# Four chained attention layers on one core: pieces of work moved between slots, and three tiles of one sum given to PE

## The chip, the cores and the metric

One core of a Trainium2 chip runs one program on 8 images. The metric is the device time of the execution in microseconds (us); lower is better. Before the change three runs took 3123.68, 3125.5 and 3131.82 us.

## The reference, cut to what matters

Each image (256 channels, 32x32 = 1024 positions) passes through four layers, numbered 0 to 3.

```python
# layer 0: group norm (32 groups), q, k, v; per head a 32x32 attention over channels
attn = softmax(einsum('bhcn,bhdn->bhcd', q, k) * 32 ** -0.5); x = x + proj(attn @ v)
# layer 1: one head, 32 channels of q and k, 128 of v, 1024x1024 attention over positions
o = einsum('oi,bihw->bohw', Wo, softmax(q^T k) applied to v) * gamma + x
# layers 2 and 3: group norm (8 groups), 8 heads of 32 channels, 1024x1024 attention per head
attn = softmax(q^T k * 32 ** -0.5); out = proj(attn @ v) + bias
# layer 2 adds its input, layer 3 adds its normalised input
```

All is float32. The softmax's maximum over each row is computed, split into two bfloat16 halves and subtracted inside the score product.

## The kernel before, in words

**Data.** The images go through one after the other. `xa` holds the image in layers 0 to 2, `scratch` in HBM is its copy between layers 1 and 2 (`save`, L640; `reload`, L643), `xb` the one that becomes layer 3's input. `Q` and `K` hold per head three stacked parts of 32 rows (high, high, low; and high, low, high), so that one fp32r product of 96 rows gives the float32 score, and 8 more rows of `Q` for the maxima.

**Groups.** Layers 2 and 3 have 4 groups each per image: 4 heads times one half (512) of the queries; layer 1 has 2. `LAST3` (4) is layer 3 of the last image. A group has 8 steps (one tile of 128 keys each) of 4 heads, that is 32 slots. In a slot PE makes one score tile of 128x512 (L1244) in one of two PSUM banks, ACT turns it into `prob` with exp (L874); after four slots PE multiplies the step's four tiles by v into the values bank (L1269), one step behind the scores. The softmax's sums: POOL adds the step's tiles into `acc` (L770), PE multiplies `acc` by ones (L1289) in `finish`. Tiles from `pooled(layer, g)` on are not added by POOL: `finish` multiplies them by ones itself (L1285), all of them before it waits for `acc`. `invert` (DVE) and `scale` (POOL, L748) follow.

**Maxima.** Ahead of a group's scores its row maxima are needed: 32 more score products (L1213; `max`) into three PSUM banks, each reduced by DVE (L997), then `split` on DVE (L1003 to L1011) and `maxrow`: a product on PE (L1220), a copy on ACT (L848) and a DMA that puts the rows into `Q` (L686). The first score of the group waits for it (L1236). They are laid beside the slots of the group before.

**Pieces.** Everything else is a piece: `side` products with a side bank of PSUM each (two banks in turn), `stats`, `norm`, `power`, `apply` of the group norms, `stack`, `save`, `load`, `store`. A q or k piece is `("side", layer, "qk", m, i)`: four PE products in two halves (`begin` and `side`, L1157), ACT's `hi` (L822), DVE's `lo` (L964), then `stack` on SP: three DMAs of 256 KB from `hi` and `lo` into `Q` or `K` (L674), four stacks for two heads groups' q and k. ACT's `hi` waits until the last stack of the same half i has landed (L815), the first maxima of a group with new stacks wait for all of them (L1204). m = 0, 1 are the early pieces, m = 2, 3 the late ones. `side(layer, "mean")` (L1064) is the product that spreads the moments over the group norm's groups: DVE's `stats` and `norm`, then ACT's moments (L836) in `norm`, then this product, then three DVE operations (L937), POOL's `power` (L727), ACT's `apply` (L794).

**Order.** `group_sequence` writes the order by hand. An entry is (layer, g, pieces with their slot, maxima). Maxima (layer, g, start, stop, low, high) are spread over slots low to high, `rows(layer, g, slot)` is a maxrow. `spread(first, last, pieces)` deals cut pieces evenly over slots; `at` gives slots one by one; `gap` is a stretch without scores. `plans` unrolls this into one list per turn, and every engine runs its own part of this list in its order, with semaphores between them. Turns: image 0 up to layer 1 and layer 2's first maxima (`first`), image 0's layer 2 with image 1's layers 0 and 1 between (`second`), `third` (one group), six times `steady`, `last`.

Of the kernel before, what the change touches and what calls it, by code (L numbers as in the profile page):

```python
# [16 lines left out]
T = C // P  # L17
# [4 lines left out]
NQ = N // QW  # L22
KC = N // P
# [12 lines left out]
LAST3 = 4  # L36
# [33 lines left out]
def normalise(layer):  # L70
    return ([("stats", layer, t, i) for t in range(T) for i in range(NQ)]
            + [("norm", layer), ("side", layer, "mean"), ("power", layer)]
            + [("apply", layer, t, i) for t in range(T) for i in range(NQ)])
# [7 lines left out]
def side(layer, what, n):  # L81
    return [("side", layer, what, i) for i in range(n)]
# [14 lines left out]
def after_layer1(rest=True):  # L97
    more = split_operand(2, 0) + split_operand(2, 1) + side(2, "v", KC // 2)
    return side(1, "out", T * NQ) + [("save",)] + normalise(2) + (more if rest else [])


def chunks(piece):

    if piece[0] != "side":
        return 1
    return {"qk": T, "v": T, "v0": 2, "v1": 2, "out": 1 if piece[1] == 1 else T, "gram": KC, "keys": T, "mix": T}.get(piece[2], 1)


def beside(pieces, others):

    return [x for i, piece in enumerate(pieces)
            for x in [piece] + others[i * len(others) // len(pieces):(i + 1) * len(others) // len(pieces)]]


def cut(pieces):

    return [x for piece in pieces for x in [("begin", c) + piece[1:] for c in range(chunks(piece) - 1)] + [piece]]


def spread(first, last, pieces):  # L120

    pieces = cut(pieces)
    return [(first + (last - first) * (2 * i + 1) // (2 * len(pieces)), x) for i, x in enumerate(pieces)]


def group_sequence():
    end = LAST_PIECE
    out2, out3 = side(2, "out", T * NQ), side(3, "out", T * NQ) + [("store", 3)]
    out1 = after_layer1(False)
    early2, late2 = (split_operand(2, m) + split_operand(2, m + 1) for m in (0, 2))  # L130
# [4 lines left out]
    def at(slots, pieces):  # L135
        return [*zip(slots, pieces)]

    def gap(pieces):
        return (None, None, pieces, [])

    def rows(layer, g, slot):
        return (layer, g, None, None, slot, slot)
# [21 lines left out]
    def layer2_begins(pieces):  # L164
# [3 lines left out]
    early_halves, late_halves = (side(2, f"v{half}", KC // HPT) for half in range(T))  # L168
    maxima2 = [("max", 2, 0, a) for a in range(MAXIMA[2])]
    first = [gap([("load",)] + channel_attention(True) + rest0 + split_operand(1, 0) + side(1, "v", 2))] + layer1 \  # L170
        + [gap(cut(out1 + early2) + beside(cut(side(2, "v", KC // 2)), maxima2) + [("split", 2, 0), ("maxrow", 2, 0)])]
    chain0 = channel_attention(True)[len(normalise(0)):] + rest0 + split_operand(1, 0) + side(1, "v", 2)
    second = [(2, 0, [(0, ("load",))] + spread(0, 14, late2)
               + at((9, 10, 11, 12, 13, 15, 16, 18, 19, 20, 21), normalise(0)) + spread(22, 32, chain0[:6]),
               [(2, 1, 0, 32, 0, 23), rows(2, 1, 27), (2, 2, 0, 8, 24, 31)]),
              (2, 1, spread(0, 26, chain0[6:]),
               [(2, 2, 8, 32, 0, 17), rows(2, 2, 19), (1, 0, 0, 8, 24, 27), rows(1, 0, 31), (1, 1, 0, 8, 28, 31)]),
              (1, 0, [], [rows(1, 1, 3), (2, 3, 0, 8, 0, 7)]),
              (1, 1, [], [(2, 3, 8, 16, 0, 7)]),
              (2, 2, at((12, 13, 14, 15, 16), out1[:T * NQ + 1])  # L180
               + at((17, 17, 18, 18, 19, 21, 24, 28, 29, 30, 31), out1[T * NQ + 1:]),
               [(2, 3, 16, 32, 0, 15), rows(2, 3, 19)]),
              (2, 3, spread(0, 14, early2) + spread(14, end, early_halves),
               [(2, 0, 0, 32, 14, 29), rows(2, 0, 31)])]
    third = [(2, 0, [(0, ("reload",))] + spread(0, 14, late2) + spread(14, 18, late_halves) + spread(18, end, out2),
              [(2, 1, 0, 32, 0, 23), rows(2, 1, 27), (2, 2, 0, 8, 24, 31)])]
    steady = (layer2(True, True)
# [2 lines left out]
                   (3, 1, 16, 24, 24, 31)]),  # L190
                 (1, 0, [], [(3, 1, 24, 32, 0, 7)]),
                 (1, 1, [], [rows(3, 1, 3), (3, 2, 0, 8, 0, 7)]),
                 (3, 1, at((12, 13, 14, 15, 16), out1[:T * NQ + 1])
                  + at((17, 17, 18, 18, 19, 21, 24, 28, 29, 30, 31), out1[T * NQ + 1:]),
                  [(3, 2, 8, 32, 0, 23), rows(3, 2, 27), (3, 3, 0, 8, 24, 31)]),
                 (3, 2, spread(0, 20, early2), [(3, 3, 8, 32, 0, 23), rows(3, 3, 27), (2, 0, 0, 8, 24, 31)]),
                 (3, 3, spread(0, end, side(2, "v", KC // 2)),
                  [(2, 0, 8, 32, 0, 23), rows(2, 0, 27), (2, 1, 0, 8, 24, 31)]),
                 (2, 0, spread(0, 14, late2) + spread(SCALED, end, out3),
# [2 lines left out]
            for x in (("side", LAST3, "out", ot * NQ + i), ("store", LAST3, ot * NQ + i))]  # L202
    half_out4 = len(out4) // NQ
    early4, late4 = (split_operand(LAST3, m) + split_operand(LAST3, m + 1) for m in (0, 2))
# [2 lines left out]
                [(3, 1, 8, 32, 0, 23), rows(3, 1, 27), (3, 2, 0, 8, 24, 31)]),  # L207
               (3, 1, at((1, 2, 3, 4, 5, 8, 11, 15, 16, 17, 18), normalise(LAST3)),
                [(3, 2, 8, 32, 0, 23), rows(3, 2, 27), (3, 3, 0, 8, 24, 31)]),
               (3, 2, spread(0, 20, early4), [(3, 3, 8, 32, 0, 23), rows(3, 3, 27), (LAST3, 0, 0, 8, 24, 31)]),  # L210
               (3, 3, spread(0, end, side(LAST3, "v", KC // 2)),
                [(LAST3, 0, 8, 32, 0, 23), rows(LAST3, 0, 27), (LAST3, 1, 0, 8, 24, 31)]),
               (LAST3, 0, spread(0, 14, late4) + spread(SCALED, end, out3),
# [85 lines left out]

def pooled(layer, g):  # L300

    return KC - 1 if layer != 2 and g > 0 or layer == LAST3 or (layer, g) == (2, 1) else KC


# [1036 lines left out]
```

## Time and profile before

| | |
|---|---|
| median of three runs | 3125.5 us |
| the profiled execution, and its span | 3135.67 us, 3133.9 us |
| busy: PE, POOL, DVE, ACT | 2853.4, 2187.9, 1857.8, 1553.1 us |
| PE, costliest lines (busy) | L1244 scores 1085.1, L1213 maxima 834.3, L1269 values 577.8 us |
| POOL, L770 sums | 1721.4 and 312.6 us |
| DVE, L997 maxima | 1411.3 us |
| DMA queue | 148.56 MB, 31.2% of 16 engines |

Times are from the start of the span. A slot's time is taken from the start of its score on PE. The profile's list of waits has for every engine and line what ended its idle time, the total, the number of times and the longest. The clock is TensorE's granted clock: 1.00 is 2.4 GHz, 0.50 is 1.2 GHz.

### The profile page before, as it was taken

The page shows a single profiled execution, that of the slowest core. Times are in us where ns is not written, and L with a number is a line of the kernel's source. Part 1 is how long each engine was busy: PE and PEld are TensorE (multiplying, and loading weights), DVE is VectorE, ACT ScalarE, POOL GpSimd, SP SyncE. Part 2 cuts the span into 40 slices and gives each one's busy share as a digit, 9 for nine tenths or more (in the row PEclk, how much of TensorE's full clock was granted, in tenths as well). Part 3 has the DMA queues.
Part 4 walks back from the last instruction along what each step waited for, and adds up shares of the span by engine and source line. Part 5 has one row for each costly group of instructions (what it writes and reads, how often), then busy time and mean ns, then how long its engine had stood idle before and what let it go on. Part 6 is the DMA issues. An engine that isn't in the chain of part 4 may idle for free.

```text
span 3133.9 us, 36186 instructions
## 1 busy us (share of the span) xinstructions
PE 2853.4 (91%) x13136; PEld 1415.3 (45%) x13136; DVE 1857.8 (59%) x3293; ACT 1553.1 (50%) x2794; POOL 2187.9 (70%) x748
## 2 busy tenths in 40 slices
PE   6668979999999989999999999999899998999997
PEld 4235434554445444454445544454344544444442
DVE  1254547566674666656675666756666566767672
ACT  1224445455564455544554545545556445555554
POOL 3215657677785777768776777867777586798877
PEclk8779889999999999999999999999999999999999
DMA  2160044333340334321343323413334123333330
GB/s 69 28 83 12 16 61 69 39 49 51 46 84 13 42 56 69 56 42 25 43 83 43 52 35 47 89 23 43 56 42 83 26 42 42 56 56 43 42 57 15
DMA packets 74388, 150.87 MB, mean 48 GB/s; under 512 B 9121, under 2 KB 10657, under 8 KB 74210
## 3 DMA queue, kind: packets, MB, share of 16 engines
q1 hardware_dynamic: 74210, 148.56, 31.2%
q8 instruction: 104, 1.70, 0.3%
q14 instruction: 74, 0.61, 0.1%
HBM read 20.46 MB, written 16.78 MB: 12 GB/s over the span
## 4 chain that ended last, share of the span: by engine, by line
PE 64%; DMA 9%; ACT 8%; DVE 7%; POOL 6%; issue 3%; SPq 2%; ACTq 0%; POOLq 0%; DVEq 0%
PE psum L1244 14%; PE psum L1269 11%; PE psum L1213 10%; POOL acc L770 6%; PE psum L1188 5%; PE psum L1157 5%; DMA Q<-lo 5%; PE psum L1165 4%; ACT prob L874 4%; PE psum L1265 3%; DVE maxpart L997 3%; DMA K<-hi 2%; PE psum L1090 2%; PE psum L1289 2%; DMA Q<-max_rows 2%
## 5 line engine op out<-in xcount | busy, mean ns | idle before, releaser
L997 DVE TENSOR_REDUCE maxpart<-psum 128x1 f32<-128x512 f32 x2176 | 1411.3, 684 | 857.3 <-PE psum L1213 835.0
L770 POOL TENSOR_TENSOR acc<-acc,prob 128x2048 f32<-128x2048 f32 (+1 forms) x447 | 1721.4, 3851 | 233.5 <-ACT prob L874 194.2
L874 ACT ACTIVATE prob<-psum 128x512 f32<-128x512 f32 x2176 | 1225.1, 596 | 1012.2 <-PE psum L1244 971.8
L1244 PE MATMUL psum<-Q,K 104*128 104x512 f32 x2048 | 1085.1, 532 | 77.8 <-ACT prob L874 55.2
L1213 PE MATMUL psum<-K,Q 96*128 96x512 f32 x2048 | 834.3, 411 | 72.4 <-DMA K<-hi 60.0
L1244 PEld LDWEIGHTS psum<-Q,K 104*128 104x128 f32 x2048 | 393.7, 193 | 780.6 <-ACT prob L874 447.6
L770 POOL TENSOR_TENSOR acc<-prob 128x2048 f32<-128x2048 f32 (+1 forms) x80 | 312.6, 3907 | 586.6 <-PE psum L1289 457.8
L1269 PE MATMUL psum<-prob,vT 128*32 128x512 f32 x4096 | 577.8, 624 | 0.0
L1213 PEld LDWEIGHTS psum<-K,Q 96*128 96x128 f32 x2048 | 401.3, 196 | 208.3 <-issue 132.4
L1269 PEld LDWEIGHTS psum<-prob,vT 128*32 128x32 f32 x4096 | 100.6, 110 | 205.6 <-ACT prob L874 122.9
L1157 PE MATMUL psum<-ha,wqkv_sb 128*128 128x512 f32 x288 | 152.0, 619 | 9.9 <-ACT ha L794 9.9
L1188 PE MATMUL psum<-att,wp_sb 128*128 128x512 f32 x256 | 131.1, 600 | 3.4 <-POOL att L748 3.4
L748 POOL TENSOR_TENSOR att<-att,turned_sums 128x512 f32<-128x512 f32 x80 | 102.1, 1276 | 28.9 <-DVE turned_sums L1025 28.9
L1157 PE MATMUL psum<-hb,wqkv_sb 128*128 128x512 f32 x224 | 120.0, 623 | 0.0
L964 DVE SCALAR_TENSOR_TENSOR lo<-psum,cols_sb,hi 128x512 fp32r<-128x512 f32 x64 | 48.1, 751 | 121.3 <-ACT hi L822 121.3
L1265 PE MATMUL psum<-prob,products 128*128 128x512 f32 x256 | 118.8, 608 | 0.0
L1289 PE MATMUL psum<-acc,ones 128*32 128x512 f32 x640 | 86.1, 610 | 15.3 <-POOL acc L770 15.3
L853 ACT COPY att<-psum 128x512 f32<-128x512 f32 x80 | 47.0, 587 | 88.3 <-PE psum L1265 52.8
L1021 DVE STREAM_TRANSPOSE turned_sums<-psum 128x512 f32<-128x512 f32 x80 | 56.5, 707 | 53.0 <-PE psum L1289 52.8
L822 ACT ACTIVATE hi<-psum,cols_sb 128x512 fp32r<-128x512 f32 x64 | 44.0, 688 | 80.3 <-DMA Q<-lo 50.4
L964 DVE SCALAR_TENSOR_TENSOR lo<-psum,hi 128x512 fp32r<-128x512 f32 x64 | 44.2, 690 | 66.5 <-ACT hi L822 66.1
L1265 PEld LDWEIGHTS psum<-prob,products 128*128 128x128 f32 x256 | 47.5, 192 | 61.7 <-issue 59.9
(117 smaller groups left out, 1970.7 us busy)
## 6 DMA issues: line engine op xcount, KB each, us to landing
Q<-hi SPq DMA_DIRECT2D x128, 256.0 KB
K<-hi SPq DMA_DIRECT2D x128, 256.0 KB
Q<-lo SPq DMA_DIRECT2D x64, 256.0 KB
K<-lo SPq DMA_DIRECT2D x64, 256.0 KB
xa<-in_x SPq DMA_DIRECT2D x8, 1024.0 KB, 8.4
scratch<-xa SPq DMA_DIRECT2D x8, 1024.0 KB, 4.0
xb<-scratch SPq DMA_DIRECT2D x8, 1024.0 KB, 4.9
out<-hb SPq DMA_DIRECT2D x7, 1024.0 KB, 5.7
```

Source lines behind the costliest of these rows:

```text
L748: pool.tensor_tensor(dst, dst, turned_sums[:, :, :].rearrange("p a c -> p (a c)"), ALU.mult).then_inc(group_done, 1)
L770: pool.tensor_tensor(total, first if a == 1 else total, this, ALU.add).then_inc(added, 1)
L874: act.activation(prob[STEP_STARTS.slot(b, start)][:, j, :], score_bank[(SCORES.rank[b.n][e] - 1) % SCORE_BANKS], ACT.Exp, scale=1.0 if lay ...
L997: dve.tensor_reduce(maxpart[layer][:, a // NQ, a % NQ:a % NQ + 1], bank, AX_X, ALU.max).then_inc(max_free, 1)
L1157: ins = pe.matmul(side_bank, wqkv_sb[layer][:, t, o:o + P], normed[layer][:, t, part], start=(t == 0), stop=(t == T - 1))
L1165: ins = pe.matmul(side_bank[:, a * width:(a + 1) * width], src[:, t, kt * P:(kt + 1) * P], w[:, t, o:o + width], start=(t == 0), stop=(t = ...
L1188: ins = pe.matmul(side_bank, w[:, t, ot * P:(ot + 1) * P], src[:, t, part], start=(t == 0), stop=(t == T - 1))
L1213: pe.matmul(max_bank[(r - 1) % MAX_BANKS], left, right, start=True, stop=True).then_inc(max_full, 1)
L1244: pe.matmul(score_bank[(r - 1) % SCORE_BANKS], left, right, start=True, stop=True).then_inc(score_full, 1)
L1265: ins = pe.matmul(values_bank, vT1[:, kt, :], slot[:, j, :], start=(kt == 0), stop=(kt == KC - 1))
L1269: ins = pe.matmul(values_bank[head_rows(j), :], vT[layer][:, s, head * DH:(head + 1) * DH], slot[:, j, :], start=(s == 0), stop=(s == KC - 1),
L1289: ins = pe.matmul(side_bank[head_rows(j), :], ones[:, :], acc[:, 0 if layer == 1 else j, :], start=(not own), stop=True, tile_position=(0, ...
```

## The change

Four things are moved in the hand-written order, and one function is changed.

- **Turn `first`**: ahead of the first maxima now stand all of layer 2's v pieces and the first late q piece with its stack; between the maxima three more stand (of m = 2 and 3) instead of v, and the last one (m = 3, i = 1) between `split` and `maxrow`, its stack behind it.
- **Turn `second`**: group (2,0) has no late pieces any more, and the normalisation of image 1 begins at slot 6 instead of 9. In (2,1) layer 0's chain and layer 1's pieces end at slot 23 instead of 26, the first maxima of layer 1 stand at slots 27 to 30 instead of 24 to 27, those of (1,1) move into (1,0). The maxima of (2,3) move one group later (8 in (1,1), 24 in (2,2)). In (2,3) early pieces and v halves end at slot 18, the maxima stand at 17 to 30 instead of 14 to 29.
- **`steady`**: in (3,1) layer 1's four output pieces and `save` stand one slot later, the means' product at slot 23 instead of 21, `power` at 25 instead of 24; in (3,2) the early pieces are dealt over slots 1 to 15 instead of 0 to 20. In the last image's (3,2) over 0 to 14.
- **`pooled`**: 5 instead of 7 for the last group of all, so that `finish` sums its tiles 5, 6 and 7 on PE.

```diff
     first = [gap([("load",)] + channel_attention(True) + rest0 + split_operand(1, 0) + side(1, "v", 2))] + layer1 \
-        + [gap(cut(out1 + early2) + beside(cut(side(2, "v", KC // 2)), maxima2) + [("split", 2, 0), ("maxrow", 2, 0)])]
+        + [gap(cut(out1 + early2 + side(2, "v", KC // 2) + late2[:2]) + beside(cut(late2[2:6]), maxima2)
+               + [("split", 2, 0)] + cut(late2[6:7]) + [("maxrow", 2, 0), late2[7]])]
     chain0 = channel_attention(True)[len(normalise(0)):] + rest0 + split_operand(1, 0) + side(1, "v", 2)
-    second = [(2, 0, [(0, ("load",))] + spread(0, 14, late2)
-               + at((9, 10, 11, 12, 13, 15, 16, 18, 19, 20, 21), normalise(0)) + spread(22, 32, chain0[:6]),
+    second = [(2, 0, [(0, ("load",))]
+               + at((6, 7, 8, 9, 10, 12, 14, 17, 18, 19, 20), normalise(0)) + spread(22, 32, chain0[:6]),
                [(2, 1, 0, 32, 0, 23), rows(2, 1, 27), (2, 2, 0, 8, 24, 31)]),
-              (2, 1, spread(0, 26, chain0[6:]),
-               [(2, 2, 8, 32, 0, 17), rows(2, 2, 19), (1, 0, 0, 8, 24, 27), rows(1, 0, 31), (1, 1, 0, 8, 28, 31)]),
-              (1, 0, [], [rows(1, 1, 3), (2, 3, 0, 8, 0, 7)]),
-              (1, 1, [], [(2, 3, 8, 16, 0, 7)]),
+              (2, 1, spread(0, 23, chain0[6:]),
+               [(2, 2, 8, 32, 0, 17), rows(2, 2, 19), (1, 0, 0, 8, 27, 30), rows(1, 0, 31)]),
+              (1, 0, [], [(1, 1, 0, 8, 0, 3), rows(1, 1, 7)]),
+              (1, 1, [], [(2, 3, 0, 8, 0, 7)]),
               (2, 2, at((12, 13, 14, 15, 16), out1[:T * NQ + 1])
                + at((17, 17, 18, 18, 19, 21, 24, 28, 29, 30, 31), out1[T * NQ + 1:]),
-               [(2, 3, 16, 32, 0, 15), rows(2, 3, 19)]),
-              (2, 3, spread(0, 14, early2) + spread(14, end, early_halves),
-               [(2, 0, 0, 32, 14, 29), rows(2, 0, 31)])]
+               [(2, 3, 8, 32, 0, 23), rows(2, 3, 27)]),
+              (2, 3, spread(0, 10, early2) + spread(10, 18, early_halves),
+               [(2, 0, 0, 32, 17, 30), rows(2, 0, 31)])]
...
-                 (3, 1, at((12, 13, 14, 15, 16), out1[:T * NQ + 1])
-                  + at((17, 17, 18, 18, 19, 21, 24, 28, 29, 30, 31), out1[T * NQ + 1:]),
+                 (3, 1, at((13, 14, 15, 16, 17), out1[:T * NQ + 1])
+                  + at((17, 17, 18, 18, 19, 23, 25, 28, 29, 30, 31), out1[T * NQ + 1:]),
...
-                 (3, 2, spread(0, 20, early2), [(3, 3, 8, 32, 0, 23), rows(3, 3, 27), (2, 0, 0, 8, 24, 31)]),
+                 (3, 2, spread(1, 15, early2), [(3, 3, 8, 32, 0, 23), rows(3, 3, 27), (2, 0, 0, 8, 24, 31)]),
...
-               (3, 2, spread(0, 20, early4), [(3, 3, 8, 32, 0, 23), rows(3, 3, 27), (LAST3, 0, 0, 8, 24, 31)]),
+               (3, 2, spread(0, 14, early4), [(3, 3, 8, 32, 0, 23), rows(3, 3, 27), (LAST3, 0, 0, 8, 24, 31)]),
...
 def pooled(layer, g):
 
+    if (layer, g) == (LAST3, T * NQ - 1):
+        return KC - 3
     return KC - 1 if layer != 2 and g > 0 or layer == LAST3 or (layer, g) == (2, 1) else KC
```

`out1` is layer 1's four output pieces, `save` and layer 2's normalisation (4 stats, norm, mean, power, 4 applies).

## Rows read from the trace of the kernel before

**Rows 1.** The page, part 1: busy us, share of the span, instructions.
```profile
PE 2853.4 (91%) x13136; PEld 1415.3 (45%) x13136; DVE 1857.8 (59%) x3293; ACT 1553.1 (50%) x2794; POOL 2187.9 (70%) x748
```
**Rows 2.** Waits of PE, whole span: total us, times, longest us.
```profile
PE psum L1213 <- DMA K<-hi: 60.0, 10, 15.1
PE psum L1244 <- ACT prob L874: 58.4, 120, 3.0
PE psum L1064 <- ACT mv L836: 29.8, 10, 12.0
```
**Rows 3.** Timeline of PE, turn 3: start us, us, work [idle before <-releaser].
```profile
741.92 0.36 PE L1064 MATMUL psum<-mv,const_sb 128*128 128x4 f32 x2 [2.12 <-ACT mv L836]
...
788.13 0.77 PE L1213 MATMUL psum<-K,Q 96*128 96x512 f32 x1 [4.68 <-DMA K<-hi]
```
**Rows 4.** Timeline of PE, images 0 and 1.
```profile
176.17 2.35 PE L1213 MATMUL psum<-K,Q 96*128 96x512 f32 x4 [15.08 <-DMA K<-hi]
...
314.54 1.19 PE L1213 MATMUL psum<-qk 96*128 96x512 f32 x2 [5.77 <-DMA qk<-K]
...
428.88 1.19 PE L1213 MATMUL psum<-K,Q 96*128 96x512 f32 x2 [11.32 <-DMA K<-hi]
```
**Rows 5.** Timelines of POOL and PE at the end of the span.
```profile
3096.40 23.30 POOL L770 TENSOR_TENSOR acc<-acc,prob 128x2048 f32<-128x2048 f32 x5
...
3119.75 1.93 PE L1289 MATMUL psum<-acc,ones 128*32 128x512 f32 x8 [5.87 <-POOL acc L770]
```
**Rows 6.** Timeline of PE, finish of (3,1) in turn 3.
```profile
763.19 1.07 PE L1285 MATMUL psum<-prob,ones 128*32 128x512 f32 x8
764.07 1.04 PE L1289 MATMUL psum<-acc,ones 128*32 128x512 f32 x8
```
**Rows 7.** Windows: length, then busy us (instructions) of each engine, clock, DMA share, GB/s.
```profile
759.66:788.13 28.47, 23.27 (x110) 10.41 (x109) 17.76 (x31) 13.88 (x25) 22.41 (x6) 0.99 0.86 112
836.67:863.90 27.23, 26.43 (x114) 12.27 (x110) 18.87 (x30) 13.52 (x25) 18.18 (x5) 1.00 0.95 116
2905.77:2935.08 29.31, 23.52 (x110) 10.34 (x109) 17.58 (x31) 14.02 (x25) 27.44 (x8) 0.99 0.84 108
...
787.41:794.23 6.82, 6.10 (x21) 3.21 (x22) 2.77 (x4) 2.37 (x4) 4.75 (x2) 0.50 0.02 2
```
**Rows 8.** Timeline of ACT, (2,0) of turn 3.
```profile
845.28 0.69 ACT L822 ACTIVATE hi<-psum,cols_sb 128x512 fp32r<-128x512 f32 x1 [3.71 <-DMA Q<-lo]
```
**Rows 9.** Windows of whole groups; the engines are PE, PEld, DVE, ACT, POOL.
```profile
832.13:874.90 42.77, 41.30 (x182) 19.12 (x181) 28.65 (x47) 21.30 (x38) 32.10 (x9) 1.00 0.67 89
3021.79:3051.13 29.34, 28.85 (x149) 12.28 (x149) 22.49 (x39) 18.45 (x34) 21.01 (x6) 1.00 0.06 18
...
713.44:753.62 40.18, 35.89 (x152) 15.67 (x150) 29.94 (x55) 20.66 (x38) 37.05 (x17) 0.96 0.08 28
```
**Rows 10.** Timeline of ACT around the moments, (3,1) of turn 3.
```profile
741.11 0.67 ACT L836 ACTIVATE mv<-mv 128x1 f32<-128x1 f32 x2 [3.03 <-DVE mv L913]
741.68 2.35 ACT L874 ACTIVATE prob<-psum 128x512 f32<-128x512 f32 x4
```
**Rows 11.** Timeline of POOL, behind power.
```profile
744.57 9.26 POOL L770 TENSOR_TENSOR acc<-acc,prob 128x2048 f32<-128x2048 f32 x2
```
**Rows 12.** Windows of images 0 and 1: the gap's wait, (2,0), (2,2), behind (2,3)'s gate.
```profile
159.00:176.17 17.17, 2.08 (x5) 1.21 (x5) 0.75 (x1) 0.69 (x1) 0.00 (x0) 0.50 0.95 112
...
202.85:251.86 49.01, 43.26 (x176) 21.91 (x176) 32.05 (x57) 26.78 (x49) 29.01 (x13) 0.89 0.58 81
...
356.36:396.44 40.08, 35.76 (x136) 13.81 (x134) 19.90 (x39) 21.60 (x40) 36.97 (x17) 0.85 0.08 28
...
428.88:459.34 30.46, 25.15 (x125) 13.81 (x126) 20.79 (x36) 11.50 (x20) 22.75 (x5) 0.89 0.05 14
```
**Rows 13.** Timeline of DVE, the gap's maxima.
```profile
180.36 16.83 DVE L997 TENSOR_REDUCE maxpart<-psum 128x1 f32<-128x512 f32 x28 [0.91 <-PE psum L1213]
```
**Rows 14.** Timeline of SP, first issues of layer 1's stacks behind a maxrow.
```profile
304.52 1.22 SPq L666 DMA_DIRECT2D qk<-hi  x2
```

## The prediction

> **What bounds the kernel now.** TensorE is busy 91% of the span [rows 1]. A share says nothing about single stages, so I read next for whom PE waited: 60.0 us in 10 waits for K's last stacked piece, 58.4 us in 120 for softmax tiles, 29.8 us in 10 for the moments ahead of the means' product [rows 2]. PE's own timeline places them. The six middle images repeat one pattern: a wait of 2.12 us ahead of the means' product and one of 4.6 to 4.7 us ahead of the first maxima of the next layer's group 0, (3,2) slot 24; the last image has the second of the two as well [rows 3, 7]. Images 0 and 1 hold the long ones, 15.08, 5.77 and 11.32 us [rows 4]. At the end PE waits 5.87 us for POOL's sums [rows 5]. PE is the bound between the waits, so the sum is made wait by wait. The windows below are cut at a group's first score.
>
> **The tail.** POOL's five last additions take 23.30 us from 3096.40, 4.66 each, and PE's last acc products start behind them at 3119.75 [rows 5]. Two additions go: POOL ends at 3110.4. PE's last values end near 3112.8, and it now sums three tiles instead of one, 0.88 us each (763.19 to 764.07 [rows 6]): 2.6 us. The acc products start at 3115.5 without a wait and run at 0.88 instead of 1.93: everything behind them is 5.1 us earlier, and a little of the low clock that stretched the last output products may go too. **-5.5 us** (-3 to -7).
>
> **Early q and k pieces, (3,2) of the middle images.** The 4.68 us are a wait for data. Four stacks of 768 KB lie between the first issue at 759.66 and the first maximum at 788.13: 28.47 us at 112 GB/s, DMA share 0.86. The late pieces of (2,0), spread over 14 slots as the early ones will be, run at 116 GB/s and 0.95 [rows 7]. The transfer can't be shortened, only its gap closed: 3.15 MB at 116 GB/s are 27.1 us, 1.3 less. The first issue moves little, since the first piece's second half stays in slot 2; the 0.76 us for which its first half waited at slot 0 is spent on slot 1's score instead. I give 0.8 for this and 0.4 for what comes earlier upstream (next paragraph): **-2.5 us** an image.
> What of the 4.68 us stays, changes place: ACT's hi of the fourth piece waits for the second stack's landing and stands in ACT's queue ahead of exponentials. In (2,0) ACT was held 3.71 us that way at 845.28 [rows 8], and PE lost little (41.30 busy of 42.77 [rows 9]), because finish and a forced piece kept it busy. In (3,2) PE has less to do there; I expect it held some 2.8 us at slots 15 to 16 and again 3 at the maxima (an estimate, on which the sum does not rest). The end is set by the stream. Bounds: 0, if the gap in the stream stays, and -7.7: the 4.68 us, and half of the 6.1 us that it runs at 1.2 GHz behind them (788.13 to 794.23 [rows 7]). Near the first, for the stream's rows say so. Six images: **-15**.
> In the last image the second half moves to slot 1, 0.9 us earlier, and its stretch, 29.31 us at 108 GB/s [rows 7], has 2.1 to close: **-3**.
>
> **The means' product, two slots later.** The diff moves PE's instruction, but ACT's moments (norm) keep slot 19. They run at 741.11 and only behind them the exponential at 741.68 [rows 10]. A score needs the exponential two before it, so PE, freed of the product, stops a score later until 742.3, when it took up its scores before too. The wait changes its name, from the moments to the tiles of prob. The output pieces a slot later save 0.6 of 1.18 us (POOL's scaled att comes when it came), the fourth passes behind a values step: 0.4 net, counted above. Cost: DVE now takes the product behind the last maximum and the four operations of the split, so POOL's power, queued ahead of the two additions of 4.63 us that ended at 753.83 [rows 11], holds these about 2.3 us. PE needs them at 764.07 [rows 6], 8 us behind that: hidden. Without this cover, 2.3 us an image.
>
> **Image 0, the gap.** In the 17.17 us ahead of the maxima PE does 2.08 us of work, at 1.2 GHz [rows 12]. All v products and a qk piece go there, some 10 to 12 us: hidden if they end by 176.2. Among the maxima (28 in 16.83 us [rows 13]) stand two lo operations in place of v, and a third piece ahead of the maxrow product: +1.8 and +0.9, less 1.5 because the first maxima no longer start at half speed. **+1.2** (-1 to +4).
> **(2,0) behind it**, 49.01 us, loses the late pieces. A half piece costs 0.76 us: (2,0) at 832.13 takes 42.77 us, with 16 halves more than the last image's (LAST3,1), 29.34, and 1.2 of idle [rows 9]. Eight are 6.1 us. With them go ACT's and DVE's waits for stacks, of the 5.75 us in which PE was not busy [rows 12] say 3.1, and 1.3 of half speed (mean clock 0.89). **-10.5**; -5 if x's load, now behind a stack, and the normalisation three slots earlier give new waits, -13 if all idle goes.
> **(2,1)**: the last stack of layer 1 has seven slots instead of two ahead of its maxima, and 14 issues of 0.6 us, the first at 304.52, set its landing [rows 14]. Of 5.77 us about 2.2 stay: -3.5. Eight maxima of 0.24 us leave for (1,0): -1.9; the split then ends just ahead of maxrow: +1. **-4.5** (-1 to -8).
> **(2,2)** takes eight maxima more, but runs at a mean clock of 0.85 now; the like group at 713.44, with all 32, takes 40.18 us at 0.96 against its 40.08 [rows 9, 12]. Less eight of 0.24, plus some clock: **-1** (-3 to +2).
> **(2,3)**: its stream has no gap to close, so its gate stays at 428.88; but three slots, a values step and three v halves (2 + 2.3 us) pass ahead of it instead of behind, where 30.46 us lay [rows 12]. DVE's floor there, 32 maxima of 0.60 [rows 13], is 19.2, and the split and row DMA behind it stay. **-4.5** (-1 to -7).
>
> **Sum**: -5.5 - 15 - 3 + 1.2 - 10.5 - 4.5 - 1 - 4.5 = -42.8 us. The profiled execution took 3135.7 us (its span 3133.9), 10 above the median of 3125.5; so 3092.9 in its terms, and 3083 for the median.
>
> **Where the clock speaks against it.** After the 4.68 us wait PE runs 6.8 us at 1.2 GHz [rows 7]. Cut in two, the wait may give two such stretches. The Trainium skill (TensorE: Matmul & The Clock Gate, HAM oscillation) says that work in bursts between DMA waits is throttled anew at each burst, to half speed. The trace agrees in direction. By that rule the split wait brings rival (a) below.
>
> **Rivals.** (a) Slower: the middle images then have three stops (the score behind the moments, slot 16, the maxima). If each draws 6.8 us at half speed, 20.5 us against 10.2 now, half of it lost, that is 5.1 more in 7 images, 36 us, with the gate unmoved; the rest keeps -24.8: +11, 3137. It decides from 3.6 us an image. For it: the 6.8 us stretch. Against: half speed ahead of a gate that DMA sets costs nothing. 4%. (b) The stream doesn't close up, as ACT's order holds the third and fourth pieces: middle and last images give 0, 3101. The rows of (2,0) speak against it. 17%. (c) Images 0 and 1 find new waits (x behind the stack, split ahead of maxrow): gap +3, (2,0) -6, (2,1) -2, (2,3) -2, that is 12.3 less: 3095. 17%. (d) Better: the stop at the gate gets too short for a low clock, 3 us in 7 images: 3062. 14%. (e) The moved pieces only rename waits everywhere and the tail alone pays: 3120, 4%. The forecast itself 44%.
> The range takes in (b), (c), (d) and the units' bounds: 3061 to 3108. Under 0.3% (9.4 us) is what this kernel's measurement can't tell from nothing. Faster by more, all but (a) and (e): 0.92; same 0.04; slower 0.04.
>
> **What would show it.** Right: K's wait in PE's list falls from 60 to 25 to 35 us and ACT's for Q's stacks grows by some 2 us an image; the moments' wait falls under 18 us while that for tiles of prob grows by about as much; from first issue to first maximum in (3,2) it is 27 us; image 0's (2,0) takes 38 us; the 5.9 us wait for acc is gone. Wrong: that stretch still 28.5 us; two low clocks in (3,2); the gap's first maxima past 178; acc late for the group after the norm.

## The result and the profile after

The changed kernel takes 3090.4 us (median of six runs, 3085.0 to 3097.0) against 3125.0 of the kernel before beside it: ratio 0.9882, 95% interval 0.9863 to 0.9900. A second series on another occasion gave 3086.0 against 3128.5, ratio 0.9864 (0.9847 to 0.9882). The forecast was 3083 with the range 3061 to 3108.

The first profiled execution of the changed kernel has a span of 3095.3 us, 38.6 less than before; that of the second series 3085.1, 48.8 less. The profiled execution before was 10 us longer than its series' median, the first one after 7 us, so the medians tell the gain (35 and 43 us) and the profiles where it lies. To read them by stage I cut both timelines of PE at the first score of each group, as in the prediction. Durations in us:

| stage | forecast | before | after | second profile |
|---|---|---|---|---|
| up to the first score, same instructions | 0 | 89.8 | 87.1 | 84.9 |
| (1,1) with the gap | +1.2 | 100.4 | 105.6 | 105.0 |
| (2,0) | -10.5 | 49.0 | 39.9 | 39.9 |
| (2,1), (1,0), (1,1) | -4.5 | 104.5 | 98.7 | 98.7 |
| (2,2) | -1 | 40.1 | 40.6 | 40.7 |
| (2,3) | -4.5 | 62.9 | 62.3 | 61.7 |
| (3,1), six middle images | 0 | 240.3 | 239.2 | 243.3 |
| (3,2), six middle images | -15 | 259.0 | 239.9 | 236.0 |
| (3,2), last image | -3 | 43.5 | 41.5 | 40.4 |
| from the last group's first score | -5.5 | 52.4 | 48.3 | 45.2 |
| sum of those that the forecast moves, against before | -42.8 | | -35.0 | -44.3 |

The two profiles of one kernel differ by up to 4.1 us in one row. In (3,1) that is TensorE's clock alone: PE is idle 24.2 us in both, and runs 20 us at 1.2 GHz in the first and 34 in the second. In (3,2) it is PE's idle time, 18.4 and 14.1 us. Single groups differ less between executions, but enough to matter for a small row: with the same instructions the old (2,3) took 62.9 to 64.4 us in four profiles (before, experiments one, two and four), the new one 60.7 to 62.3 in five (the two of the changed kernel, three, six and seven). So the sum says more than its parts.

PE's busy time hardly moves; what goes is its waiting. The page's first part of the changed kernel, to be held against [rows 1]:

```profile
PE 2858.6 (92%) x13152; PEld 1411.0 (46%) x13152; DVE 1857.5 (60%) x3293; ACT 1552.5 (50%) x2794; POOL 2178.9 (70%) x746
```

Its list of PE's waits (total us, times, longest), to be held against [rows 2], and under it that of ACT, both over the whole span:

```profile
PE psum L1247 <- ACT prob L877: 75.7, 125, 2.7
PE psum L1216 <- DMA K<-hi: 18.5, 10, 3.7
PE psum L1067 <- ACT mv L839: 18.4, 3, 11.7
PE psum L1247 <- DMA Q<-max_rows: 13.9, 16, 5.2
```
```profile
ACT hi L825 <- DMA Q<-lo: 108.8, 45, 6.9
```

The wait for K's last piece falls from 60.0 to 18.5 us (11.8 in the second profile), that for the moments from 29.8 to 18.4, and that for tiles of prob grows by 17.3. ACT waited 85.1 us for Q's stacks before.

### The profile page after: what moved, and what is told of

It reads as the page before. It is cut to its first block, busy times and chain, and to the rows that moved or that the text cites. A ratio compares the mean times of both kernels' runs of the same rounds, so it can differ in the third digit from the quotient of the medians.

```text
span 3095.3 us, 36215 instructions
## 1 busy us (share of the span) xinstructions
PE 2858.6 (92%) x13152; PEld 1411.0 (46%) x13152; DVE 1857.5 (60%) x3293; ACT 1552.5 (50%) x2794; POOL 2178.9 (70%) x746
## 4 chain that ended last, share of the span: by engine, by line
PE 64%; DMA 12%; ACT 8%; DVE 7%; POOL 3%; issue 3%; SPq 2%; ACTq 0%; POOLq 0%; DVEq 0%
PE psum L1247 15%; PE psum L1272 11%; PE psum L1216 10%; DMA Q<-lo 7%; PE psum L1191 6%; PE psum L1160 5%; ACT prob L877 4%; PE psum L1168 4%; PE psum L1268 4%; DVE maxpart L1000 3%; POOL acc L773 3%; DMA K<-hi 3%; PE psum L1093 2%; DMA Q<-max_rows 2%; DVE stats L909 2%
## 5 line engine op out<-in xcount | busy, mean ns | idle before, releaser
L1216 PE MATMUL psum<-K,Q 96*128 96x512 f32 x2048 | 838.5, 413 | 35.4 <-DMA K<-hi 18.5
L1292 PE MATMUL psum<-acc,ones 128*32 128x512 f32 x640 | 87.3, 617 | 12.7 <-POOL acc L773 8.6
L730 POOL TENSOR_TENSOR rstd<-gvar,half_power 128x2 f32<-128x2 f32 x24 | 16.8, 699 | 93.8 <-DVE gvar L942 93.8
```

The costliest lines, as they stand in the source:

```text
L1216: pe.matmul(max_bank[(r - 1) % MAX_BANKS], left, right, start=True, stop=True).then_inc(max_full, 1)
```

## Experiments

Each gives its edit, then what was on record, then what came. In each the kernel before ran on the same chip, 3126.0 us in the first four, 3128.5 in the next four, 3129.0 in the last three.

**One: early pieces alone**, in the kernel before.

```diff
-  (3, 2, spread(0, 20, early2), [(3, 3, 8, 32, 0, 23), rows(3, 3, 27), (2, 0, 0, 8, 24, 31)]),
+  (3, 2, spread(1, 15, early2), [(3, 3, 8, 32, 0, 23), rows(3, 3, 27), (2, 0, 0, 8, 24, 31)]),
...
-  (3, 2, spread(0, 20, early4), [(3, 3, 8, 32, 0, 23), rows(3, 3, 27), (LAST3, 0, 0, 8, 24, 31)]),
+  (3, 2, spread(0, 14, early4), [(3, 3, 8, 32, 0, 23), rows(3, 3, 27), (LAST3, 0, 0, 8, 24, 31)]),
```


> The kernel before with only the early q and k pieces dealt over slots 1 to 15 (steady) and 0 to 14 (last image). My theory (the end is set by the data stream of four stacks, whose gap closes, and a shorter wait leaves less time at 1.2 GHz): first issue to first maximum in (3,2) falls from 28.5 to 27.3 us, the group takes 3 us less in each of the 7 images, the total falls by 18 to 24 us, ACT's hi is held about 2.5 us for the fourth piece. Rival (half of it comes from the output pieces and the means' product that stand one and two slots later): the group gains under 1.5 us an image, the total under 11 us. Rival (the clock eats it): two low clocks in (3,2) and the total within 5 us of before.

Measured: 3111.3 us, ratio 0.9948 (0.9931 to 0.9966), 16 us. The six groups (3,2) took 234.7 us, 24.3 less, the last 3.4 less; PE's wait for K was 36.3 us. So the early pieces are the largest part, and with 27.7 us by stage larger than the forecast's 18. The total is less than the 18 to 24 us expected of this run: its profiled execution is 5 us shorter than its median and the one before 10 us longer than its own, so the stages say more than the medians bear out. The rival that gave half of the gain to the output pieces is out: they are not moved here.

**Two: the means' product alone**, in the kernel before.

```diff
-  (3, 1, at((12, 13, 14, 15, 16), out1[:T * NQ + 1])
-   + at((17, 17, 18, 18, 19, 21, 24, 28, 29, 30, 31), out1[T * NQ + 1:]),
+  (3, 1, at((13, 14, 15, 16, 17), out1[:T * NQ + 1])
+   + at((17, 17, 18, 18, 19, 23, 25, 28, 29, 30, 31), out1[T * NQ + 1:]),
```


> The kernel before with only the six (3,1) groups changed: output pieces and save one slot later, means' product at slot 23, power at 25. My theory (PE's stop is ACT's norm in front of the exponentials, so the wait is only renamed): waits for the moments fall by about 12 us and waits of L1244 for prob grow by as much; (3,1) takes 0.2 to 0.5 us less an image at the same clock, the total falls by 0 to 3 us, not measurable. Rival (the product's wait is really removed): 2.1 us an image, the total falls by 12 us or more.

Measured: 3126.0 us, ratio 0.9997 (0.9986 to 1.0008): nothing. PE's waits in it, over the whole span:

```profile
PE psum L1244 <- ACT prob L874: 75.8, 129, 2.9
PE psum L1213 <- DMA K<-hi: 58.8, 10, 15.1
PE psum L1064 <- ACT mv L836: 17.1, 4, 11.7
```

Against [rows 2] the moments' wait loses 12.7 us and that for prob gains 17.4: a change of name, as expected.

**Three: images 0 and 1 alone.** The edit is the change's first hunk whole, from `first` to the end of `second`; in its kernel the pairs of lines are these and those of `second`:

```diff
-        + [gap(cut(out1 + early2) + beside(cut(side(2, "v", KC // 2)), maxima2) + [("split", 2, 0), ("maxrow", 2, 0)])]
+        + [gap(cut(out1 + early2 + side(2, "v", KC // 2) + late2[:2]) + beside(cut(late2[2:6]), maxima2)
+               + [("split", 2, 0)] + cut(late2[6:7]) + [("maxrow", 2, 0), late2[7]])]
...
```

> The kernel before with only the turns first and second changed (images 0 and 1). My theory, from the trace of after: gap +5, (2,0) -9, (2,1) and (1,0) together -6, (2,2) and (2,3) within 1 each; 10 us less in all up to the end of (2,3), and 10 +- 4 in the total. Rival (my forecast of 19 us was right and after's execution met a low clock by chance there): 16 us or more.

Measured: 3120.5 us, ratio 0.9980 (0.9969 to 0.9991), 6 us. By stage: gap with (1,1) 105.8, (2,0) 37.7, (2,1) 74.7, (2,3) 60.7 us, in sum with (1,0), (1,1) and (2,2) 10.7 less. Of the 19.3 us forecast there about half comes, as was expected of this run after the first profile; its rival, a low clock by chance, is out.

**Four: the tail alone.**

```diff
+    if (layer, g) == (LAST3, T * NQ - 1):
+        return KC - 3
```

> The kernel before with only the last group's tiles 5 and 6 moved from POOL to PE. My theory: POOL's last additions end 9.3 us earlier, PE's acc products start behind its own 2.6 us without a wait for POOL, the last group takes 4 to 5 us less, and the total falls by about 5 us, at the edge of what can be measured. Rival (the end is set by ACT's values copy and the output stores): under 2 us.

Measured: 3121.2 us, ratio 0.9983 (0.9971 to 0.9994), 5 us. PE's timeline at its end (start, us, work, idle before):

```profile
3106.14 2.76 PE L1287 MATMUL psum<-prob,ones 128*32 128x512 f32 x24
3108.72 1.04 PE L1291 MATMUL psum<-acc,ones 128*32 128x512 f32 x8
```

The acc products follow without a wait. The four parts give 16 + 1 + 6 + 5 = 28 us by their ratios, the whole 37 and 43 by its two: no sign that the parts take anything from each other. Whether they help each other stays open; each interval is 3 to 6 us to either side.

**Five: the changed kernel once more**, for the comparisons below.

> The changed kernel itself, beside its variants on one chip, so that their differences are read against it. Both theories: about 3090 us, ratio to the kernel before 0.986 to 0.990, with the stages of its first profile: steady (3,2) near 240 us for the six, (3,1) near 239, the gap with (1,1) near 105, (2,3) near 62, tail near 48.

Measured: 3086.0 us, its stages as in the table's last column; there (3,1) is 4 us above the 239 expected, (3,2) 4 below 240 and the tail 3 below 48.

**Six: the moments two slots later as well**, in the changed kernel.

```diff
-  + at((17, 17, 18, 18, 19, 23, 25, 28, 29, 30, 31), out1[T * NQ + 1:]),
+  + at((17, 17, 18, 18, 21, 23, 25, 28, 29, 30, 31), out1[T * NQ + 1:]),
```


> The changed kernel with the steady means' normalisation called two score slots later (21 instead of 19), so that ACT's moments of the mean stand behind two more exponentials. Theory 1 (the stop of 2 to 2.7 us at score slot 22 of every steady (3,1) group is ACT held in order by the mean's moments, which wait for PE's transposed sums, with exponentials queued behind them): that stop goes, the six (3,1) groups take about 227 instead of 239 us, the waits for ACT's probabilities fall by about 12 us, total about 3078. Theory 2 (the stop is only one of several equal ones, and PE is then held by the mean's own product at slot 23 or by a later exponential): (3,1) stays within 4 us of 239, the wait for ACT's mv is over 25 us, total 3087 to 3093.

Measured: 3092.3 us (3087.3 to 3093.3), ratio 0.9885 (0.9869 to 0.9901), against 0.9864 for the changed kernel beside it: no gain, and if anything 6 us more, with intervals that overlap. That is the second theory's total; its (3,1) within 4 us of 239 and its wait for the moments of over 25 us were missed narrowly (233.9 and 24.8). Its waits of PE:

```profile
PE psum L1247 <- ACT prob L877: 60.4, 121, 2.2
PE psum L1067 <- ACT mv L839: 24.8, 9, 11.6
PE psum L1216 <- DVE maxpart L1000: 18.6, 34, 1.5
```

The tiles' wait falls by 16.3 us against the 76.7 of the same kernel without the edit, and 6.4 come back at the moments, 4.9 at the maxima that stand behind DVE's part of the norm. PE is idle 0.8 us less in each (3,1), 4.6 in six. In its profile the six took 233.9 us against 243.3, but most of that is the clock: by the groups' mean clocks 10 us of the six ran at 1.2 GHz against 34. The runs' times show no gain.

**Seven: one late piece back behind the row maxima's product**, in the changed kernel's gap.

```diff
-  + [("split", 2, 0)] + cut(late2[6:7]) + [("maxrow", 2, 0), late2[7]])]
+  + [("split", 2, 0), ("maxrow", 2, 0)] + cut(late2[6:]))]
```


> The changed kernel with only this moved back: in the gap before image 0 the second of the two late q/k pieces that the change put between the first maxima stands behind the transposition of the row maxima. Theory 1 (each piece between the maxima holds DVE for 1.5 to 2 us, and its stack's DMAs stand in front of the row maxima's DMA, for whose landing PE waits 5.2 us): the gap with (1,1) is 1.5 to 3 us shorter than 105, and (2,0) loses less than 1 of it, total about 3088. Theory 2 (the gap is set by the landing of the first K stacks, and the piece only moves the waiting): gap and (2,0) together within 0.5 us.

Measured: 3098.9 us (3096.3 to 3100.8), ratio 0.9908 (0.9892 to 0.9924): 13 us slower than the changed kernel beside it. The gap with (1,1) is 3.0 us shorter, as the first theory said, and (2,0) 3.6 longer, which it did not. PE's and DVE's timelines in its (2,0):

```profile
211.19 0.80 PE L1216 MATMUL psum<-K,Q 96*128 96x512 f32 x1 [4.65 <-DVE maxpart L1000]
```
```profile
209.85 0.69 DVE L909 BATCH_NORM_STATS2 stats<-xa 128x6 f32<-128x512 f32 x1 [4.81 <-DMA xa<-in_x]
```

PE waits for a PSUM bank of the maxima, DVE's reductions stand behind the next image's statistics, and those wait for x, whose transfer was issued at 200.85 behind the moved piece's stack. What the gap gains, the next image's load takes back. Gap and (2,0) together take 145.5 us, as in the changed kernel's two profiles (145.5 and 144.8): the second theory's number, but not its mechanism, for the gap did get shorter and the wait is for x, not for the first K stacks. Nearly all of the 12 us by which this profile is longer than the changed kernel's second lies behind, in instructions that were not moved: (2,1) and (1,0) 5.2 us and the end 3.1, with 14 and 7 us more at 1.2 GHz; the groups from `third` on 5.6, where PE is idle 7.6 us longer and runs 7 us less at 1.2 GHz; (2,2) is 2.4 shorter. Why is open, so this run does not show what the piece's place is worth to the total.

**Eight: K's pieces ahead of Q's**, in the changed kernel.

```diff
-    early2, late2 = (split_operand(2, m) + split_operand(2, m + 1) for m in (0, 2))
+    early2, late2 = (split_operand(2, m + 1) + split_operand(2, m) for m in (0, 2))
-    early3, late3 = (split_operand(3, m) + split_operand(3, m + 1) for m in (0, 2))
+    early3, late3 = (split_operand(3, m + 1) + split_operand(3, m) for m in (0, 2))
...
-  for i in range(2):
-      pe.wait_ge(stacked[i], b.last(STACKED[i], [("stack", layer, m, i) for m in ms], e))
+  m = 0 if layer == 1 else g // NQ * 2
+  needed = [(m, 0), (m, 1)] if layer == 1 else [(m, 0), (m + 1, 1)] if g % NQ == 0 else [(m, 1)]
+  for m, i in needed:
+      pe.wait_ge(stacked[i], b.last(STACKED[i], [("stack", layer, m, i)], e))
```

The last image's pieces are swapped in the same way, PE's wait for the normalised input moves to the piece that is now first, and the condition around `needed` lets the second group of a pair wait too.

> The changed kernel with K's pieces cut and stacked before Q's for every pair of images after the first, and the first group's maxima waiting for three of the four early stacks (both of K, the first of Q) instead of all four. Theory 1 (behind the move of the pieces the first maxima of a group still wait for the last landing of four stacks, which follow each other through one queue): the first maxima start about 6 us earlier after the first issue (27 to 21 us), the six steady (3,2) groups take about 228 instead of 240 us and (2,3) up to 6 less, total 3072 to 3082. Theory 2 (what is left in (3,2) is ACT and DVE, which are held in order by the pieces' own low parts, not the landing): the gate opens earlier, PE stops as long at later slots, (3,2) within 4 us of 240, total 3086 to 3094.

Measured: 3071.4 us (3052.1 to 3079.5), ratio 0.9815 (0.9792 to 0.9838); once more beside the last two 3071.4, 0.9813 (0.9793 to 0.9834). That is 15 us faster than the changed kernel beside it. The six (3,2) took 219.7 us, 16 to 20 less, and the wait for K is gone from PE's list. (`m` is Q's piece, `m + 1` K's; a group with g even now waits for three stacks, the next one for the fourth.) Windows of this group in turn 3, of before, after and this kernel (length, then PE, PEld, DVE, ACT, POOL busy, clock, DMA share, GB/s):

```profile
753.62:797.30 43.68, 37.66 (x168) 17.25 (x164) 25.80 (x43) 22.65 (x41) 28.72 (x8) 0.92 0.58 74
```
```profile
747.53:787.68 40.15, 36.81 (x169) 16.21 (x165) 25.79 (x43) 22.66 (x41) 31.15 (x8) 0.96 0.64 81
```
```profile
741.45:778.39 36.94, 35.34 (x169) 15.69 (x165) 25.75 (x43) 22.54 (x41) 26.30 (x7) 1.00 0.70 88
```

PE's idle time goes 6.0, 3.3, 1.6 us and its busy time falls with the clock's rise from 0.92 to 1.00. ACT's last wait for a stack in the turn after, and PE's first maximum there (a line without a bracket has no wait ahead of it):

```profile
1123.84 0.69 ACT L825 ACTIVATE hi<-psum,cols_sb 128x512 fp32r<-128x512 f32 x1 [2.27 <-DMA K<-hi]
```
```profile
1133.70 0.50 PE L1248 MATMUL psum<-Q,K 104*128 104x512 f32 x1
1134.05 0.40 PE L1217 MATMUL psum<-K,Q 96*128 96x512 f32 x1
```

ACT is held as long as ever (109.5 us over the span for 108.8 and 107.4), but the first maxima (1134.05) have no wait ahead of them. They start 23.8 to 25.9 us after the first issue, for 26.0 to 27.4 in the changed kernel; the 21 us of the first theory are not reached, because PE gets there only then with its own work, and yet (3,2) lies below its 228. Both edits are needed by the order of issue: with Q first the last stack issued is K's second, which is among the three awaited, and with all four awaited the last landing counts in any order. That is argued; neither was run alone. Not all of it reaches the total: (2,1) of image 0 takes 77.5 us for 72.0, with the same idle time of PE and 21 us at 1.2 GHz for 8.

**Nine: the maxima of (2,3) two slots earlier**, in the kernel of eight.

```diff
-               [(2, 0, 0, 32, 17, 30), rows(2, 0, 31)])]
+               [(2, 0, 0, 32, 15, 28), rows(2, 0, 29)])]
```


> The variant with K's pieces ahead of Q's, and image 1's group (2,3) starts the 32 maxima of the next image two score slots earlier (15 to 28 instead of 17 to 30) with the transposition of the row maxima at 29 instead of 31. Theory 1 (with three stacks instead of four awaited, (2,3) has its first maxima ready before slot 17, and its last wait, 4.5 us at slot 31, is only for the row maxima's way through DVE, PE and a DMA, which nothing covers): that wait falls to under 1.5 us, (2,3) takes about 55.5 instead of 58.9 us, total 3 us less than the kernel it builds on. Theory 2 (the first maxima are held by the landing again as soon as they are asked for earlier): PE stops 2 to 3 us at slot 15, (2,3) stays within 1 us of 58.9.

Measured: 3067.5 us (3066.5 to 3074.6), ratio 0.9809 (0.9792 to 0.9826): not to be told from eight. Its (2,3) took 57.0 us against 58.9 and 60.6 in eight's two profiles, all of it clock: PE is idle 13.7 us in it against 13.5. Neither theory fits: PE stops 1.2 us ahead of the first maxima, and the two waits at the end take 4.9 us in place of the 1.5 expected. The waits for the split and for the rows' DMA, in its timeline of PE:

```profile
440.00 0.38 PE L1224 MATMUL psum<-ident_bf,maxsplit 128*8 128x128 bf16 x4 [2.24 <-DVE maxsplit L1014]
...
444.67 0.47 PE L1248 MATMUL psum<-Q,K 104*128 104x512 f32 x1 [2.63 <-DMA Q<-max_rows]
```

**Ten: nine with the moments at slot 21.**

> As the one before, and with the steady means' normalisation called at slot 21 instead of 19. Theory 1 (its 4.6 us less idle time of PE in the six (3,1) groups is real): 3 to 6 us less than the one before. Theory 2 (what it takes from one wait comes back in the mean's own product): within 2 us of it.

Measured: 3066.7 us (3065.2 to 3073.7), ratio 0.9804 (0.9787 to 0.9821): as nine, the second theory's total. PE's idle time in the six (3,1) is again 4.8 us less than in nine (19.6 for 24.4), but they take 1.7 us more, with 24 us at 1.2 GHz for 17. Eight's second run:

> The variant with K's pieces ahead of Q's once more, beside two that build on it. Both theories: 3066 to 3078 us, (2,3) near 59 us, six steady (3,2) near 220 us.

Measured: 3071.4 us, as said; (2,3) 60.6 and (3,2) 220.0 us.

## Why the prediction was right, and where its steps were not

**The bound** (right). PE's waits were the right unit. Of what would show it, K's wait fell below its 25 to 35 us (18.5), the moments' to 18.4 for "under 18", while the tiles' grew by 17.3, more than the 11.4 that the moments lost. ACT's wait for stacks grew by 23.7 us for "some 2 an image", image 0's (2,0) takes 39.9 us for 38, and the wait for acc at the end is gone. Of the signs of being wrong one came in one of six groups: two stretches at 1.2 GHz in (3,2) of turn 4.

**The tail** (right, -5.5; -4.2 and -7.2 measured, 5 alone). POOL's three additions and PE's sums behind them in the changed kernel, to be held against [rows 5]:

```profile
3061.89 13.96 POOL L773 TENSOR_TENSOR acc<-acc,prob 128x2048 f32<-128x2048 f32 x3
```
```profile
3078.33 2.76 PE L1288 MATMUL psum<-prob,ones 128*32 128x512 f32 x24
3080.90 1.04 PE L1292 MATMUL psum<-acc,ones 128*32 128x512 f32 x8
3085.31 6.72 PE L1191 MATMUL psum<-att,wp_sb 128*128 128x512 f32 x8 [3.37 <-POOL att L751]
```

Three tiles cost 2.76 (two of them moved, for tile 7 was PE's before), as three times 0.88 said, and the acc products start 4.4 us earlier in the group. POOL is done at 3075.85, 2.5 us ahead of PE's own sums: by these rows one tile fewer for PE would do about as well (not tried). The spread between the two profiles is the output products' clock: the low clock that "may go" was still there in the first, where the last products take 6.72 us, and gone in the second, where they take 3.67.

**(3,2), early pieces** (right in mechanism, size too small). Forecast -2.5 an image, measured -3.2 and -3.8, and -4.05 in the run with this part alone; last image -3 against -2.0, -3.1 and -3.4. From the first issue to just ahead of the first maximum, in turn 4:

```profile
1116.52:1143.44 26.92, 24.74 (x109) 10.75 (x108) 17.82 (x31) 13.84 (x25) 19.31 (x5) 0.94 0.96 117
```

The stream runs at 117 GB/s. The first maximum starts 27.4 us behind the first issue in this turn and 26.0 to 27.0 in the five others, for 28.4 to 28.5 before, where I had worked out 27.1: the stream closed up as forecast, and rival (b) is out. The wait did fall apart as I said:

```profile
1132.59 0.69 ACT L825 ACTIVATE hi<-psum,cols_sb 128x512 fp32r<-128x512 f32 x1 [2.57 <-DMA Q<-lo]
```
```profile
1133.82 0.50 PE L1247 MATMUL psum<-Q,K 104*128 104x512 f32 x1 [1.41 <-ACT prob L877]
...
1143.95 0.47 PE L1216 MATMUL psum<-K,Q 96*128 96x512 f32 x1 [1.06 <-DMA K<-hi]
```

ACT was held 2.57 us, but PE only 1.41 and then 1.06 (0.4 to 1.4 and 0.7 to 3.0 over the six turns; estimated 2.8 and 3). The first maximum stands 32.3 us behind the group's first score for 34.5 before, in both profiles: 2.2 us of the forecast's 2.5. What I mis-sized lies behind it, 7.6 and 7.1 us for 8.7. The time at 1.2 GHz fell from 6.3 us a group to 3.4 and 4.0; I had priced nothing of the 6.1 us at 1.2 GHz [rows 7] and left it in the far bound. The term lacked it.

**The rule on the clock** (rival (a)). The split wait gave no more microseconds at half speed: (3,1) and (3,2) together ran 9.6 us an image at 1.2 GHz before, 6.8 and 9.6 after in the two profiles, and not the 20.5 that the rival asked for. The Trainium skill (TensorE: Matmul & The Clock Gate, HAM oscillation) says that work in bursts between DMA waits is throttled anew at each burst; its example has DMA waits of some 3 to 5 us. Before the change the wait of 4.6 to 4.7 us had a stretch at 1.2 GHz with it in every image. After it, in the first profile, the two shorter waits had one behind each of them in turn 4, one in all in four turns, and none in turn 7, where they were 0.55 and 1.96 us. Only the kernels without the second wait (eight to ten) ran most of these groups at 1.00. So the rule's direction holds here, its "at each burst" for the long wait alone.

**The means' product** (right). Nothing was forecast and nothing came. PE's timeline and ACT's in turn 4, against [rows 3, 10], and POOL's against [rows 11]:

```profile
1099.77 0.50 PE L1247 MATMUL psum<-Q,K 104*128 104x512 f32 x1 [2.65 <-ACT prob L877]
```
```profile
1098.57 0.66 ACT L839 ACTIVATE mv<-mv 128x1 f32<-128x1 f32 x2 [3.25 <-DVE mv L916]
1099.14 2.25 ACT L877 ACTIVATE prob<-psum 128x512 f32<-128x512 f32 x4
```
```profile
1103.27 0.70 POOL L730 TENSOR_TENSOR rstd<-gvar,half_power 128x2 f32<-128x2 f32 x1 [2.53 <-DVE gvar L942]
```

The product no longer waits, and the score of slot 22 stops instead, 2.65 us, for an exponential that stands behind the moments in ACT's order. POOL is held 2.53 us as forecast (2.3), hidden. The Trainium skill (PSUM — Partial Sum Buffer, Engine vs sequencer instructions) calls the queues of ScalarE, VectorE and GpSimdE strict FIFO; the rows of ACT and POOL agree, and none here tests VectorE's. The edit moved the wrong instruction: the one that holds the queue is ACT's. Moving that one too (experiment six) takes 16 us out of the tiles' wait, but 11 come back at the next two links, DVE's and the product's own. By these waits the stop belongs to a chain through DVE, ACT and PE, whose links take it over one from the other; no run removed it.

**Image 0, the gap** (+1.2 forecast, +5.2 and +4.6 measured, both past its bound of +4). The first maxima came when they were due (PE idle 0.99 instead of 15.08):

```profile
173.15 0.93 PE L1216 MATMUL psum<-K,Q 96*128 96x512 f32 x3 [0.99 <-DMA K<-hi]
```

But what I priced at +1.8, two `lo` among the maxima, cost 3.9: DVE takes 23.4 us from the first maximum to the last, of which the maxima are 19.5. It took 20.2 before, and 0.9 of these were a wait for the slow first maxima, part of the 1.5 that I had credited. These are not only DVE's 0.75 us each: DVE waits at each for ACT's `hi` and then for PE's next maximum, as its timeline shows:

```profile
185.97 3.08 DVE L1000 TENSOR_REDUCE maxpart<-psum 128x1 f32<-128x512 f32 x5 [1.23 <-PE psum L1216]
189.49 0.75 DVE L967 SCALAR_TENSOR_TENSOR lo<-psum,cols_sb,hi 128x512 fp32r<-128x512 f32 x1 [0.45 <-ACT hi L825]
```

The third piece, ahead of the rows' product, cost 1.4 for 0.9. And from that product to the first score it takes 5.8 us for 4.6, a term that I did not have: ACT makes this piece's `hi` ahead of its copy of the rows, 0.4 us of it, and the rows' DMA takes the rest. Experiment seven shows what the piece buys: behind the product it costs (2,0) 3.6 us and saves 3.0 in the gap. So its price and its gain cancel within 1 us.

**(2,0)** (-10.5; -9.1 twice) and **(2,1) with (1,0)** (-4.5; -5.8) are right within the error of a row. In (2,0) PE's idle time fell by 4.2 us for the 3.1 forecast, but the time at 1.2 GHz grew from 11 to 16 us, where I had taken 1.3 off for it. **(2,2)** (-1; +0.5 and +0.6) stays within its bounds of -3 to +2.

**(2,3)** (-4.5 forecast; -0.6 and -1.2 measured, outside its bounds of -1 to -7 in the first profile). Beside the gap this is the step that failed, and the one whose reasoning was at fault. The gate stands where I left it, 33.1 us behind the group's start for 32.4 before, and the work moved ahead did fill the wait, 3.67 instead of 11.32 us [rows 4]:

```profile
400.16 1.94 PE L1292 MATMUL psum<-acc,ones 128*32 128x512 f32 x8 [4.10 <-DVEq L970]
...
417.46 1.19 PE L1216 MATMUL psum<-K,Q 96*128 96x512 f32 x2 [3.67 <-DMA K<-hi]
...
446.73 0.77 PE L1247 MATMUL psum<-Q,K 104*128 104x512 f32 x1 [2.85 <-DMA Q<-max_rows]
```

Behind it lie 29.3 us for 30.46, where I had taken 4.3 off for the moved work. I had named what forbids that, DVE's floor of 19.2 us and the way of the rows, and had not added it up: 3.8 us until DVE starts its third maximum (a v half of 1.91 us at 1.2 GHz stands ahead of it), 19.9 for the 30 others with DVE's small waits, and 5.6 from the split to the first score of the next group. DVE's timeline at both ends:

```profile
421.25 2.51 DVE L1000 TENSOR_REDUCE maxpart<-psum 128x1 f32<-128x512 f32 x4 [1.70 <-PE psum L1216]
...
436.83 4.27 DVE L1000 TENSOR_REDUCE maxpart<-psum 128x1 f32<-128x512 f32 x7 [0.47 <-PE psum L1216]
441.14 0.19 DVE L1006 TENSOR_REDUCE maxima<-maxpart 128x16 f32<-128x32 f32 x1
```

The profile before flatters the old group a little: over the nine profiles named under the table the stretch behind the gate fell from 30.8 us on the mean (30.5 to 31.4) to 28.3 (27.7 to 29.3), 2.5 us of the 4.3 that I took, and the gate stands 0.4 later. But for the first microseconds PE was not the bound behind that gate, so work taken from it there is worth little; the gate's own time is what counts. Experiment eight moves it and gets 1 to 3.5 us, while nine, which asks for the maxima sooner, gets no less idle time. The stop of 4.10 us ahead of 400.16, where `finish` stands behind the fourth piece, is new; I take it for an effect of the denser pieces, which I had not seen either. Before, the longest stop ahead of the gate was 2.96 us, for a tile of prob.

**In sum** the range held, and that the total came within 8 us of the forecast is in part luck, for two halves erred against each other: images 0 and 1 gave 10 to 11 us of the 19.3 forecast, the middle and last (3,2) 21 to 26 of 18. Rival (c) was closer than the forecast on images 0 and 1: it named the gap (+3) and (2,3) (-2), and was wrong on (2,0) (-6). (Its terms add to 11.3 us, not the 12.3 that the prediction writes, which makes 3094.)

**The version that beats both** is that of experiment eight, 0.981 of the kernel before: it lets the gate wait for three stacks of the stream, where the change only closed the stream's gap. Nine and ten add nothing that can be told.

## What to carry to other kernels

Where a wait ends with the last of several transfers through one queue, first ask which of them the waiting instruction needs: reordering them and waiting for three instead of four brought 15 us, about what moving the pieces in (3,2) had brought (16). When a wait is cut by moving work ahead of it, add up what stands behind it on the other engines before you book the gain. Where an instruction holds an in-order engine, moving its consumer only changes the name of the wait; moving the instruction itself took 0.8 us of PE's idle time an image here, and no time that the runs can tell.

## What had not been expected of the hardware

The granted clock decides several microseconds from one execution of the same program to the next: the end of the changed kernel took 48.3 us in one and 45.2 in the other, with 7.2 us at 1.2 GHz and none, and the same idle time of PE (11.3). It also differs between like groups of one execution. In the six (3,1) of the changed kernel's first profile PE's stop of 2.65 us is the same within 0.01 us; with it the clock stayed at 2.4 GHz in turn 3, ran 3.4 us at 1.2 GHz in four turns and 6.8 us in turn 5. The groups of turns 3, 4 and 5 (columns as above, the clock third from the end):

```profile
708.98:747.53 38.55, 34.47 (x153) 15.53 (x151) 29.86 (x55) 20.54 (x38) 33.10 (x17) 1.00 0.08 29
1071.23:1110.93 39.70, 35.69 (x152) 16.35 (x151) 30.03 (x55) 20.63 (x38) 34.21 (x17) 0.96 0.08 29
1434.83:1476.01 41.18, 37.16 (x152) 17.36 (x150) 30.16 (x55) 20.85 (x38) 34.97 (x17) 0.92 0.08 27
```

The low stretch of turn 4 lies behind the stop that ends at 1099.77; the two windows cut it in half, so each shows a mean of the two levels:

```profile
1099.77:1103.20 3.43, 3.43 (x16) 1.72 (x17) 2.41 (x9) 1.52 (x3) 0.97 (x1) 0.75 0.01 2
1103.20:1106.60 3.40, 3.40 (x20) 1.92 (x18) 2.64 (x4) 2.71 (x5) 3.10 (x5) 0.75 0.00 0
```
